# The scan's first 127 sums on VectorE, and VectorE's chains as single operations in a new order

## The chip, the core and the metric

The kernel runs on one core of one Trainium2 chip. The metric is the device time of one execution in microseconds. The core has TensorE (PE, matmuls), VectorE (DVE), ScalarE (ACT), GpSimd (POOL), and SyncE (SP), which issues all DMA transfers here. Each engine works through its own queue in order; engines meet at semaphores.

## The reference

The input x is (4, 1024, 256). Two layers follow, each inside `x = x + layernorm(layer(layernorm(x)))`.

The first layer is a gated recurrence over time, per channel and batch:

```
px = x @ W_state.T + b_state;  g = sigmoid(x @ W_gate.T + b_gate)
state = tanh(px[t] + state);   out[t] = g[t] * state        # t = 0 .. 1023
```

The second is causal attention with 16 heads of 16 (queries and keys RMS-normalised per head), then a router that picks 2 of 4 experts of one to four linear maps each with GELU or SiLU, all in float32:

```
x = x + attention(rms(x));  x = x + sum over experts of weight * expert(rms(x))
```

The tanh of step t needs the state of step t - 1, so the recurrence is 1024 dependent steps on small data: 128 partitions x 8 numbers.

## The kernel before, in words

The work is cut in time into 4 chunks of 256 steps (`NCH`) and, behind the recurrence, into 16 units (`NU`) of 256 rows each; a unit of the first chunk holds 128 time steps of two batches. Units 0 and 1 need steps 0 to 127, units 2 and 3 steps 128 to 255, and so on.

**The head.** For each of 8 half-chunks n: `xin` loads x, `hst` computes LayerNorm statistics and a reciprocal root, `hsc` scales, `htr` transposes on TensorE (4 x 2 transposes), `hcp` copies PSUM to SBUF, `hpx0` and `hpx1` are the two products (state and gate), `hout0` adds the bias (px), and `hgt` and `hout1` are the gate's tanh on ScalarE. Between these stand pieces of the weights (`wl` load, `wsh` and `wsp` split in a high and a low part, `wst` store), since float32 products are made of three products of rounded parts (`PARTS`).

**The scan.** `sadd` n adds px of step n and the state of step n - 1 on GpSimd (line 2227), `stanh` n is the tanh on ScalarE (line 1387). They alternate 1023 times. In the queues they stand between the other work of their engines: `STEPS` says how many other items come before each of them.

**A unit u.** `gl` loads the gates, `pgate` multiplies gate and state on VectorE (line 1942 for the first chunk) and waits for the last tanh of the unit's rows; `ptr` transposes, `pcp` copies, `pln` and `pu` are LayerNorms on VectorE; then `qh`, `qtr`, `qhT`, `qhl`, the products `qk` and `vm`, the norm `qrs` of queries and keys, `kh`/`kt`/`kc` and `qq`/`qt`/`qc` for keys and queries, the maxima of the scores `mxm` (TensorE) and `mxr` (VectorE, line 2026), scores and exponentials `sc`/`ex`, products with values `av`, division `mgd`, output product `wo`, norm `r3`, router `gm`/`ga`/`gex`/`gb`, experts `up`/`gel`/`dn`/`da`, last LayerNorm `fin`, store `ost`.

**The order of the work** is written out by hand in tables and the program replays it. `arrange` lists all items with an engine, a cost in us and their dependences; `Plan.sequence` orders them by `PLACES` (a place in one list for every item, 4843 of them) and puts the steps of the scan between them; `Plan.run` goes through the list, gives out buffers and PSUM banks by the costs (`PINNED` fixes some banks), and leaves one order for each engine. The costs set no time on the chip; they choose buffers, and the tables fit them.

**Dummies.** `WARM` says in front of which TensorE item how many units of two 128x128 products of the identity stand (line 1579, traced at line 1563 as `PS<-ident`); 420 units in all.

**Chains on VectorE.** An item such as `pln` (line 1945 and on), `pu`, `fin`, `r3`, `hst`, `qrs`, `kh`, `qq`, `mgd`, `ga` or `gb` is several dependent VectorE instructions. Before, they are issued one behind the other, each waiting for the one before on the semaphore `link` (`step`, `rsqrt` and `stats`, lines 1806 to 1847), with nothing of another item between. An item of VectorE is thus one piece in the order.

Of the kernel before, what the change touches and what calls it, by code (L numbers as in the profile page):

```python
# [24 lines left out]
EPS_LN = 1e-5  # L25
# [3 lines left out]
SKEW = 3e-4  # L29
FINE = 4  # L30
# [12 lines left out]
           "XF": 2, "EF": 2, "EP": 2, "W": 6, "MB": 4, "mx": 1, "MT": 1, "avbank": 1, "GG": 1}  # L43
# [9 lines left out]
RATE, IDLE = 300.0, 0.222  # L53
ISSUE = {"kst": 0.58, "vst": 0.58, "mtd": 0.73, "gl": 0.64, "kts": 0.62, "vl": 0.62, "wr": 0.6, "x1l": 0.62}
# [6 lines left out]
    "wl": (19, 2, 5, 26, 89, 58, 70, 54, 307, 111, 63, 12, 53, 190, 186, 189, 192, 195, 193, 231, 220, 249, 216, 284,  # L61
        257, 262, 235, 416, 336, 329, 322, 480),
    "cbx": (6,),
    "cqk": (108,),
    "wsp": (153, 60, 72, 474, 194, 188, 202, 210, 212, 205, 252, 255, 261, 234, 342, 335, 328, 318, 437, 523, 435, 410,
        513),
    "wsh": (191, 187, 201, 209, 211, 203, 232, 228, 260, 229, 341, 317, 313, 247, 434, 431, 423, 381, 510),
    "wst": (511, 198, 299, 238, 213, 305, 275, 256, 408, 251, 345, 556, 517, 404, 499, 524, 504, 603, 527),
    "wdd": (91, 657, 237, 147),
    "xin": (1, 17, 33, 59, 68, 88, 115, 155),  # L70
    "hst": (4, 18, 35, 61, 69, 106, 123, 164),
    "hsc": (7, 9, 10, 11, 22, 24, 30, 29, 37, 41, 42, 46, 64, 78, 79, 62, 98, 85, 102, 87, 117, 116, 135, 137, 124, 132,
        130, 144, 171, 174, 165, 173),
    "htr": (8, 13, 14, 15, 23, 25, 31, 32, 38, 43, 44, 49, 80, 81, 82, 84, 99, 101, 103, 104, 133, 134, 136, 138, 148,
        150, 151, 152, 172, 175, 176, 177),
    "hcp": (16, 48, 50, 105, 110, 143, 154, 178),
# [3 lines left out]
    "hgt": (28, 34, 36, 39, 40, 45, 47, 52, 56, 65, 66, 67, 71, 74, 77, 86, 90, 93, 94, 95, 96, 112, 131, 141, 146, 149,  # L80
# [23 lines left out]
    "pcp": (206, 224, 637, 525, 1146, 1211, 1281, 1457, 1951, 2032, 2095, 2471, 3203, 2652, 3273, 3678),  # L104
    "pln": (214, 242, 659, 538, 1147, 1217, 1305, 1470, 2009, 2066, 2124, 2529, 3227, 2673, 3287, 3701),
# [3 lines left out]
    "qtr": (226, 296, 722, 574, 1181, 1241, 1373, 1543, 2021, 2119, 2370, 2569, 3261, 2767, 3378, 3751),  # L109
    "qhT": (230, 298, 724, 577, 1209, 1245, 1378, 1567, 2026, 2176, 2383, 2586, 3269, 2784, 3408, 3761),  # L110
    "qhl": (239, 312, 731, 588, 1210, 1265, 1380, 1569, 2038, 2177, 2385, 2597, 3270, 2785, 3409, 3762),
    "qk": (240, 253, 319, 337, 732, 745, 593, 616, 1215, 1229, 1287, 1313, 1448, 1473, 1582, 1634, 2045, 2071, 2225,
        2285, 2392, 2463, 2616, 2729, 3274, 3324, 2892, 2973, 3547, 3577, 3764, 3936),
    "qkc": (245, 264, 324, 343, 737, 757, 600, 625, 1216, 1230, 1295, 1314, 1460, 1474, 1584, 1636, 2046, 2078, 2255,
        2298, 2417, 2480, 2631, 2730, 3280, 3334, 2903, 2974, 3560, 3583, 3772, 3941),
    "qred": (246, 267, 333, 344, 744, 758, 601, 654, 1221, 1235, 1296, 1315, 1463, 1476, 1633, 1640, 2047, 2079, 2257,
# [3 lines left out]
    "vst": (295, 438, 854, 776, 1282, 1437, 1553, 1866, 2249, 2488, 2620, 2910, 3488, 3317, 3612, 4175),  # L120
    "qrs": (269, 346, 759, 655, 1240, 1327, 1490, 1643, 2084, 2306, 2486, 2758, 3345, 2989, 3600, 3969),
# [6 lines left out]
    "kst": (290, 310, 392, 433, 792, 816, 691, 725, 1286, 1333, 1433, 1466, 1546, 1600, 1705, 1796, 2117, 2190, 2333,  # L128
# [2135 lines left out]
```

## Time and profile before

| | us |
|---|---|
| median of 3 runs | 1461.81 (1460.68 to 1465.23) |
| the profiled execution | 1454.77 |
| its span, first to last instruction | 1453.0 |
| TensorE matmuls busy | 1407.3 (97%) |
| VectorE busy | 1096.2 (75%) |
| ScalarE busy | 883.7 (61%) |
| GpSimd busy | 312.7 (22%) |
| mean granted TensorE clock | 0.997 of full |

Busy shares count matmuls of any kind, dummies too. Recorded durations of small instructions overlap, so an instruction's start tells more than its end. In rows of the timeline a name such as `AD<-PX` is output and input tile, `x4` a count of like instructions merged in one row, and a bracket the idle time of the engine just before with what ended it.

### The profile page before, as it was taken

The numbers are of one execution on the slowest core, as the hardware profiler recorded it, in microseconds if no ns is written. First come the engines' busy times: TensorE is split into PE (matmuls) and PEld (weight loads), VectorE is DVE, ScalarE is ACT, GpSimd is POOL, SyncE is SP. The second block draws the span as 40 slices with busy tenths as digits, with TensorE's granted clock in tenths as the row PEclk, the third lists the DMA queues.
The fourth block names the chain that finished last, engine by engine and source line by source line (L and its number), as shares of the span: only waits on it lengthen the run. The fifth ranks groups of instructions, "written<-read, shape, count | busy, mean of one in ns | idle before, by whom it ended". The sixth has DMA issues, their size and how long they took to land.

```text
span 1453.0 us, 35319 instructions
## 1 busy us (share of the span) xinstructions
PE 1407.3 (97%) x13160; PEld 1169.3 (80%) x13160; DVE 1096.2 (75%) x2916; ACT 883.7 (61%) x2262; POOL 312.7 (22%) x1146
## 2 busy tenths in 40 slices
PE   9999899999999999999999999999999999999997
PEld 6478789978997688877988689867887677986797
DVE  7858777566899877778998788788899378772544
ACT  3546577567666774776676952468322886339841
POOL 3344333332133323333333200001000100001100
PEclk9999999999999999999999999999999999999999
DMA  3547766765576657646666666676566666667453
GB/s 108 167 146 232 220 209 181 226 215 155 163 230 209 200 180 202 199 141 185 214 202 193 199 199 201 203 222 208 166 194 197 207 214 180 205 207 248 150 172 120
DMA packets 242234, 278.63 MB, mean 192 GB/s; under 512 B 35088, under 2 KB 165648, under 8 KB 241808
## 3 DMA queue, kind: packets, MB, share of 16 engines
q1 hardware_dynamic: 242064, 276.38, 62.5%
q8 instruction: 105, 1.72, 0.5%
q14 instruction: 65, 0.53, 0.1%
HBM read 234.18 MB, written 43.45 MB: 191 GB/s over the span
## 4 chain that ended last, share of the span: by engine, by line
PE 70%; DVE 14%; ACT 6%; DMA 3%; issue 3%; POOL 2%; SPq 1%; ACTq 0%; DVEq 0%; POOLq 0%
PE PS L1563 65%; PE PS L1566 3%; PE PS L1646 2%; POOL AD L2227 2%; DVE mx L2026 1%; ACT PX L1387 1%; DMA KT<-ktd 1%; DVE st L1844 1%; ACT work L1494 1%; DMA QT<-MT 1%; ACT PX L1494 1%; DVE ss L1992 1%; DVE rst L1831 1%; DVE rst L1825 1%; DVE mv L1847 0%
## 5 line engine op out<-in xcount | busy, mean ns | idle before, releaser
L1387 ACT ACTIVATE PX<-AD 128x8 f32<-128x8 f32 x1023 | 221.2, 216 | 217.6 <-POOL AD L2227 210.4
L2227 POOL TENSOR_TENSOR AD<-PX 128x8 f32<-128x8 f32 x1023 | 245.7, 240 | 499.8 <-ACT PX L1387 489.5
L2026 DVE TENSOR_REDUCE mx<-PS 128x2 f32<-128x1024 f32 (+3 forms) x256 | 254.9, 1018 | 40.4 <-PE PS L1563 39.6
L1563 PE MATMUL PS<-EP,u_e_l 128*128 128x256 f32 x1024 | 194.1, 284 | 1.3 <-issue 1.2
L1494 ACT ACTIVATE work<-PS 128x1024 f32<-128x1024 f32 (+1 forms) x199 | 182.2, 958 | 13.3 <-PE PS L1563 12.5
L1563 PE MATMUL PS<-WB,work 128*128 128x192 f32 x1024 | 180.1, 330 | 0.1
L1563 PE MATMUL PS<-work,vlx 128*32 128x256 f32 (+2 forms) x2104 | 174.8, 365 | 4.8 <-ACT work L1494 1.2
L1563 PE MATMUL PS<-EP,WB 128*128 128x256 f32 x640 | 178.8, 279 | 0.0
L1531 ACT ACTIVATE work<-PS 128x512 f32<-128x512 f32 x132 | 77.3, 595 | 160.6 <-PE PS L1563 160.1
L1563 PEld LDWEIGHTS PS<-WB,work 128*128 128x128 f32 x1024 | 164.9, 190 | 3.9 <-ACT work L1531 1.1
L1563 PEld LDWEIGHTS PS<-EP,u_e_l 128*128 128x128 f32 x1024 | 160.2, 188 | 4.5 <-issue 3.1
L1563 PE MATMUL PS<-XF,WB 128*128 128x256 f32 x576 | 161.0, 280 | 0.0
L2234 POOL TENSOR_SCALAR_AFFINE_SELECT work<-work 128x512 f32<-128x512 f32 x70 | 45.6, 659 | 454.0 <-ACT work L1494 454.0
L1563 PE MATMUL PS<-KT,QT 64*128 64x512 f32 (+3 forms) x768 | 136.2, 409 | 3.2 <-DVE mx L2026 1.6
L1563 PE MATMUL PS<-QT,KT 64*128 64x256 f32 (+1 forms) x1344 | 128.2, 303 | 5.5 <-DMA KT<-ktd 2.6
L1563 PEld LDWEIGHTS PS<-QT,KT 64*128 64x128 f32 x1344 | 93.4, 186 | 49.5 <-issue 29.1
L1563 PE MATMUL PS<-ident 128*128 128x128 f32 x840 | 123.3, 286 | 6.5 <-DVE mx L2026 2.6
L1563 PEld LDWEIGHTS PS<-work,vlx 128*32 128x32 f32 (+1 forms) x2104 | 73.7, 114 | 67.5 <-issue 33.1
L2026 DVE TENSOR_REDUCE mxb<-PS 128x2 f32<-128x768 f32 (+3 forms) x128 | 104.1, 819 | 24.4 <-PE PS L1563 23.7
L1563 PEld LDWEIGHTS PS<-ident 128*128 128x128 f32 x840 | 107.1, 194 | 18.9 <-issue 6.1
L1563 PEld LDWEIGHTS PS<-EP,WB 128*128 128x128 f32 x640 | 120.2, 188 | 0.0
L1563 PEld LDWEIGHTS PS<-XF,WB 128*128 128x128 f32 x576 | 108.3, 188 | 0.2
(201 smaller groups left out, 2600.7 us busy)
## 6 DMA issues: line engine op xcount, KB each, us to landing
KT<-ktd SPq DMA_DIRECT2D x112, 512.0 KB, 4.4
WB<-wlo_e_l SPq DMA_DIRECT2D x160, 256.0 KB, 3.6
ktd<-KTs SPq DMA_DIRECT2D x32, 512.0 KB, 4.3
WB<-wlo_e_up SPq DMA_DIRECT2D x64, 256.0 KB, 3.9
WB<-wlo_e_w SPq DMA_DIRECT2D x64, 256.0 KB, 3.8
WB<-wdn_e_down SPq DMA_DIRECT2D x64, 192.0 KB, 2.9
KT<-ktd SPq DMA_DIRECT2D x48, 256.0 KB, 3.6
KT<-ktd SPq DMA_DIRECT2D x32, 384.0 KB, 3.6
```

Source lines behind the costliest of these rows:

```text
L1387: eng.activation(cur, AD[n % 2], ACT.Tanh).then_inc(of(*key), 1)
L1494: eng.activation(pt[:, :, :, q0:L], x[:, :, :, q0:L], ACT.Exp).then_inc(of(*key), 1)
L1531: eng.activation(o, x, ACT.Gelu).then_inc(of(*key), 1)
L1563: return eng.matmul(o, l, r, start=start, stop=stop, skip_group_check=skip)
L1566: return eng.transpose(o, i, ident)
L1646: ins = eng.transpose(ps[:, p // 4, 128 * (p % 4):128 * (p % 4) + 128].bitcast(F32R), QKP[:, 2 * p:2 * p + 2, :].rearrange("p h r -> p (h ...
L1825: step(eng.reciprocal(t, t))
L1831: step(eng.reciprocal(t, t))
L1844: step(eng.bn_stats(s_[:, i, :], src[:, i, :]))
L2026: eng.tensor_reduce(o, two("mxm", *a)[:, :, 0:w], AX, ALU.max, negate=True).then_inc(of(*key), 1)
L2227: eng.tensor_tensor(AD[n % 2], PX[c % 2][:, :, :, t], PX[(n - 1) // L % 2][:, :, :, (n - 1) % L], ALU.add).then_inc(of(*key), 1)
L2234: eng.affine_select(out=p, in_=p, compare_op=ALU.is_ge, fill=0.0, base=0, pattern=[[0, 2], [0, 2], [1, 128]], channel_multiplier=-1).then_ ...
```

## The change

`sadd` 1 to 127 go to VectorE (`HERE = 128`); from 128 on they stay on GpSimd. Every chain of VectorE is listed as its single operations `("op", i, ...)`, each an item with its own place in the order; each still waits for the operation before it. `OPS` gives the number of operations ahead of the last: 1336 in all. The number of instructions stays as it was, but for small details. Scratch is made private where chains may now overlap (four sets `st2`, `mv2`, `r3`, `r4`, and the statistics' own columns for the roots). `PLACES` has 6179 entries; `STEPS`, `WARM` and `PINNED` are new as well. Some costs of the planner differ.

WARM's units by place, counted from the tables:

| before which items | before | after |
|---|---|---|
| first transposes (`htr` 0) | 32 | 4 |
| the rest of the head | 29 | 68 |
| `ptr` of unit 0 | 38 | 19 |
| the rest of unit 0 | 115 | 98 |
| unit 1 | 81 | 58 |
| units 2 to 15 | 125 | 83 |
| all | 420 | 330 |

In the order of VectorE two weight pieces (`wsh` at places 187 and 191) stand ahead of the first `pgate` (196) before, and one (`wsh` at 263, `pgate` at 265) after.

```diff
+HERE = 128
+OWN = ("pln", "pu", "fin", "r3")
+OPS = {"pln": 11, "pu": 12, "fin": 11, "r3": 8, "ga": 6, "gb": 12, "qrs": 7, "kh": 3, "qq": 1, "mgd": 1, "hst": 9}
...
+RELOAD = 0.08
...
+    def chain(key, costs, us, *after, last=(), take=None, first=(), at=None):
+
+        hold = (len(costs) if at is None else at)
+        prev = [("op", 0, key[0], key[1] - 4)] if key[0] in OWN and key[1] >= 4 else []
+        for i, cost in enumerate(costs):
+            mine = take if i == hold else None
+            if i:
+                add("dve", ("op", i, *key), cost, ("op", i - 1, *key), take=mine)
+            else:
+                add("dve", ("op", 0, *key), cost, *after, seq=[*[(k[2], k[3]) for k in prev], *first], take=mine)
+        add("dve", key, us, ("op", len(costs) - 1, *key), *last, take=take if hold == len(costs) else None)
...
-        add("dve", ("hst", n), 3.66, ("xin", n), seq=hold)
+        chain(("hst", n), (1.32, 0.28, *ROOT[1:]), 0.067, ("xin", n), first=hold)
...
-            add("pool", ("sadd", n), 0.245, ("stanh", n - 1), *px)
+            add(*(("dve", ("sadd", n), 0.075) if n < HERE else ("pool", ("sadd", n), 0.245)), ("stanh", n - 1), *px)
...
-        add("dve", ("pln", u), 4.12, ("pcp", u), ("xl", u))
+        chain(("pln", u), (0.66, 0.15, *ROOT, 0.62), 0.62, ("pcp", u), last=[("xl", u)])
...
-            add("pe", ("mgt", u, g), 0.2, ("avc", u, g), mode="128",
+            add("pe", ("mgt", u, g), 0.218, ("avc", u, g), mode="128",
...
             for key in plan.order["dve"]:
+                i, key = (key[1], key[2:]) if key[0] == "op" else (None, key)
                 kind, a = key[0], key[1:]
-                if kind == "cbx":
+                sig = of(*key) if i is None else of("op", i, *key)
+                if i:
+                    v.wait_ge(*done("op", i - 1, *key))
+                elif i is None and ("op", 0, *key) in plan.items:
+                    v.wait_ge(*done("op", OPS[kind] - 1, *key))
+                if kind == "sadd":
+                    n = a[0]
+                    v.wait_ge(*done("hout0", n // 128))
+                    v.wait_ge(*done("stanh", n - 1))
+                    eng.tensor_tensor(AD[n % 2], PX[0][:, :, :, n], PX[0][:, :, :, n - 1], ALU.add).then_inc(sig, 1)
+                elif kind == "cbx":
...
                 elif kind == "r3":
                     u = a[0]
-                    c, b = divmod(u, B)
-                    v.wait_ge(*done("sqs", u))
-                    rsqrt(r3, sq2, 2, (1.0 / C,), (EPS_RMS,))
-                    v.wait_ge(link, steps[0])
-                    for x in freed(key, "HA"):
-                        v.wait_ge(*x)
-                    for s in range(2):
-                        ins = eng.tensor_scalar(HA[:, s, :], rows_of(u)[:, s, :], r3[:, s:s + 1], None, ALU.mult)
-                    ins.then_inc(of(*key), 1)
+                    o = r3[:, u % 4]
+                    if i is None:
+                        for x in freed(key, "HA"):
+                            v.wait_ge(*x)
+                        for k in range(2):
+                            ins = eng.tensor_scalar(HA[:, k, :], rows_of(u)[:, k, :], o[:, k:k + 1], None, ALU.mult)
+                        ins.then_inc(sig, 1)
+                    else:
+                        if i == 0:
+                            v.wait_ge(*done("sqs", u))
+                        root(i, o, sq2, 2, (1.0 / C,), (EPS_RMS,), r3t[:, u % 4, 0], r3t[:, u % 4, 1]).then_inc(sig, 1)
```

The other chains are rewritten in the same way as `r3`; `root` holds the eight operations of `rsqrt`, one for each i.

## Rows read from the trace of the kernel before

**Rows 1.** The page: busy us by engine, and the chain that ended last.
```profile
PE 1407.3 (97%) x13160; PEld 1169.3 (80%) x13160; DVE 1096.2 (75%) x2916; ACT 883.7 (61%) x2262; POOL 312.7 (22%) x1146
...
PE 70%; DVE 14%; ACT 6%; DMA 3%; issue 3%; POOL 2%; SPq 1%; ACTq 0%; DVEq 0%; POOLq 0%
```

**Rows 2.** Windows: stretch, length, busy PE, PEld, DVE, ACT, POOL (instructions), clock, DMA.
```profile
20.00:30.00 10.00, 9.98 (x38) 5.31 (x37) 9.38 (x32) 5.88 (x27) 3.86 (x18) 1.00 0.46 132
...
60.00:80.00 20.00, 19.20 (x61) 9.51 (x60) 11.49 (x30) 10.12 (x46) 8.14 (x37) 1.00 0.62 177
80.00:100.00 20.00, 20.00 (x152) 17.61 (x151) 11.34 (x30) 8.62 (x39) 8.17 (x31) 1.00 0.56 170
...
350.00:500.00 150.00, 143.29 (x1364) 122.34 (x1364) 133.66 (x371) 103.23 (x318) 44.39 (x168) 1.00 0.66 199
...
1400.00:1453.00 53.00, 45.35 (x354) 44.96 (x353) 22.06 (x79) 14.05 (x21) 0.00 (x0) 0.96 0.47 145
```

**Rows 3.** Identity products on TensorE: the page's group, and 80 to 100 us.
```profile
L1563 PE MATMUL PS<-ident 128*128 128x128 f32 x840 | 123.3, 286 | 6.5 <-DVE mx L2026 2.6 <-POOL ident L2186 1.6 <-ACT work L1494 1.0
...
80.00:100.00 20.00, 15.71 (x141) 1.00 0.56 170
```

**Rows 4.** The chain that ended last in order of time: start, us, what.
```profile
1.58 8.94 PE PS L1563 x64
...
73.70 10.76 PE PS L1563 x28
...
1395.55 49.82 PE PS L1563 x386
```

**Rows 5.** Timeline of one step of the scan: start, us, engine, line, operation.
```profile
20.11 0.21 POOL L2227 TENSOR_TENSOR AD<-PX 128x8 f32<-128x8 f32 x1 [0.33 <-ACT PX L1387]
...
20.35 0.22 ACT L1387 ACTIVATE PX<-AD 128x8 f32<-128x8 f32 x1 [0.32 <-POOL AD L2227]
...
20.65 0.20 POOL L2227 TENSOR_TENSOR AD<-PX 128x8 f32<-128x8 f32 x1 [0.33 <-ACT PX L1387]
```

**Rows 6.** Groups of GpSimd, 18 to 88 us: busy us, mean ns, idle before.
```profile
L2227 POOL TENSOR_TENSOR AD<-PX 128x8 f32<-128x8 f32 x126 | 27.3, 217 | 52.3 <-ACT PX L1387 42.1 <-ACT PX L1384 10.2
```

**Rows 7.** Timeline of VectorE: a chain's end, and the next chain's first two operations.
```profile
187.72 0.16 DVE L1978 TENSOR_TENSOR tv<-tv,ru 128x2 f32<-128x2 f32 x1
187.80 0.16 DVE L1817 TENSOR_SCALAR rsx<-sq 128x2 f32<-128x2 f32 x1
188.00 0.17 DVE L1821 TENSOR_SCALAR r<-rsx 128x2 int32<-128x2 int32 x1
```

**Rows 8.** Timeline of VectorE around the first pgate (L1942).
```profile
87.25 0.43 DVE L1861 CAST u_e_up<-work 128x512 fp32r<-128x512 f32 x1 [4.72 <-DMA work<-in_L_ffn_e_up]
...
90.67 0.43 DVE L1861 CAST u_e_up<-work 128x512 fp32r<-128x512 f32 x1 [2.26 <-DMA work<-in_L_ffn_e_up]
91.13 0.69 DVE L1867 TENSOR_TENSOR WB<-work,u_e_up 128x512 fp32r<-128x512 f32 x1
91.74 0.75 DVE L1942 SCALAR_TENSOR_TENSOR G<-G,PX 128x256 f32<-128x256 f32 x2
```

**Rows 9.** Groups of VectorE by form, 18 to 88 us.
```profile
L1913 DVE COPY work<-PS 128x1024 f32<-128x1024 f32 x7 | 8.4, 1219 | 1.0 <-PE PS L1566 1.0
L1844 DVE BATCH_NORM_STATS2 st<-UU 128x6 f32<-128x256 f32 x24 | 8.4, 411 | 1.7 <-DMA UU<-in_L_attn_x 1.7
L1927 DVE TENSOR_SCALAR work<-PS,bx 128x512 f32<-128x512 f32 x8 | 5.6, 746 | 8.6 <-PE PS L1563 8.6
...
L1927 DVE TENSOR_SCALAR PX<-PS,bx 128x512 f32<-128x512 f32 x6 | 4.2, 746 | 0.6 <-PE PS L1563 0.6
```

**Rows 10.** Window of VectorE alone: length, busy us.
```profile
18.00:88.00 70.00, 50.78 (x154) 1.00 0.45 130
```

**Rows 11.** Windows of TensorE: busy us, granted clock.
```profile
640.00:660.00 20.00, 17.35 (x188) 1.00 0.55 172
660.00:680.00 20.00, 19.58 (x199) 0.91 0.48 144
```

More of the change, by code:

```diff
@@ L555, in __init__ @@
     def __init__(self):
-        self.items, self.after, self.queue = {}, {}, set()
+        self.items, self.after, self.queue, self.fresh = {}, {}, set(), set()
     def add(self, engine, key, us, *after, seq=(), take=None, mode=None, kb=0.0):
@@ L662, in run @@
                     t = max(t, t1)
+                if k in self.fresh and after == k[0]:
+                    us += RELOAD
                 us *= clock(t)
@@ L852, in arrange @@
                 take = {"P2": (("mxr", u, i),), "MB": (("mxr", u, i),)}
+                if not k0:
+                    P.fresh.add(("mxm", u, i))
                 if i == 0:
@@ L962, in arrange @@
         dma(("x1l", u), 256, ("x1st", u), take={"XR": (("fin", u),)})
-        add("dve", ("fin", u), 4.11, ("da", u, "e3_out"), ("x1l", u))
+        chain(("fin", u), (0.66, 0.15, *ROOT, 0.62), 0.62, ("da", u, "e3_out"), last=[("x1l", u)])
         dma(("ost", u), 256, ("fin", u))
@@ L1895, in _ @@
                     n = a[0]
-                    c, s = divmod(n, 2)
-                    v.wait_ge(*done("xin", n))
-                    m_ = mv.rearrange("p (b s) k -> p s b k", s=2)[:, s]
-                    stats(half(n), st.rearrange("p (b s) k -> p s b k", s=2)[:, s], m_)
-                    rsqrt(r1[:, 4 * s:4 * s + 4], m_[:, :, 1], 4, (1.0,), (EPS_LN,), key)
+                    c, h = divmod(n, 2)
+                    m_, s_ = (x.rearrange("p (b s) k -> p s b k", s=2)[:, h] for x in (mv, st))
+                    if i == 0:
+                        v.wait_ge(*done("xin", n))
+                        for k in range(4):
+                            ins = eng.bn_stats(s_[:, k, :], half(n)[:, k, :])
+                    elif i == 1:
+                        for k in range(4):
+                            ins = eng.bn_aggr(m_[:, k, :], s_[:, k, :])
+                    else:
+                        ins = root(7 if i is None else i - 2, r1[:, 4 * h:4 * h + 4], m_[:, :, 1], 4, (1.0,), (EPS_LN,),
+                                   s_[:, :, 0], s_[:, :, 1])
+                    ins.then_inc(sig, 1)
                 elif kind == "hsc":
@@ L1959, in _ @@
-                    v.wait_ge(*done("xl", u))
-                    v.wait_ge(link, steps[0])
-                    eng.tensor_tensor(xr, xr, Ub, ALU.add).then_inc(of(*key), 1)
+                    b = u % B
+                    ti, xr, Ub = 2 * b, XR[place[("xl", u), "XR"]], rows_of(u)
+                    m_, s_, o = mv[:, ti:ti + 2, :], st[:, ti:ti + 2, :], r1[:, ti:ti + 2]
+                    if i is None:
+                        v.wait_ge(*done("xl", u))
+                        eng.tensor_tensor(xr, xr, Ub, ALU.add).then_inc(sig, 1)
+                    elif i == 0:
+                        v.wait_ge(*done("pcp", u))
+                        for k in range(2):
+                            ins = eng.bn_stats(s_[:, k, :], Ub[:, k, :])
+                        ins.then_inc(sig, 1)
+                    elif i == 1:
+                        for k in range(2):
+                            ins = eng.bn_aggr(m_[:, k, :], s_[:, k, :])
+                        ins.then_inc(sig, 1)
+                    elif i < 10:
+                        root(i - 2, o, m_[:, :, 1], 2, (1.0,), (4.0 * EPS_LN,), s_[:, 0, 0:2], s_[:, 1, 0:2]).then_inc(sig, 1)
+                    else:
+                        for k in range(2):
+                            ins = eng.tensor_scalar(Ub[:, k, :], Ub[:, k, :], m_[:, k, 0:1], o[:, k:k + 1], ALU.subtract, ALU.mult)
+                        ins.then_inc(sig, 1)
@@ L1972, in _ @@
-                    for i in range(2):
-                        step(eng.tensor_scalar(rows_of(u)[:, i, :], xr[:, i, :], m_[:, i, 0:1], ru[:, b, 0, i:i + 1],
-                                               ALU.subtract, ALU.mult))
-                    t_ = tv[:, ti:ti + 2]
-                    step(eng.scalar_tensor_tensor(t_, m_[:, :, 1], EPS_LN, ru[:, b, 0], ALU.add, ALU.mult))
-                    v.wait_ge(link, steps[0])
-                    eng.tensor_tensor(t_, t_, ru[:, b, 1], ALU.mult).then_inc(of(*key), 1)
+                    b = u % B
@@ new lines, in _ @@
+                    ti, xr, Ub = 2 * b, XR[place[("xl", u), "XR"]], rows_of(u)
+                    m_, s_, t_, o = mv[:, ti:ti + 2, :], st[:, ti:ti + 2, :], tv[:, ti:ti + 2], ru[:, b]
+                    if i is None:
+                        eng.tensor_tensor(t_, t_, o[:, 1], ALU.mult).then_inc(sig, 1)
+                    elif i == 0:
+                        v.wait_ge(*done("pln", u))
+                        for k in range(2):
+                            ins = eng.bn_stats(s_[:, k, :], xr[:, k, :])
+                        ins.then_inc(sig, 1)
+                    elif i == 1:
+                        for k in range(2):
+                            ins = eng.bn_aggr(m_[:, k, :], s_[:, k, :])
+                        ins.then_inc(sig, 1)
+                    elif i < 10:
+                        root(i - 2, o.rearrange("p k s -> p (k s)"), m_[:, :, 1], 4, (1.0, 1.0 + EPS_RMS), (EPS_LN, EPS_RMS * EPS_LN),
+                             s_[:, 0, 0:4], s_[:, 1, 0:4]).then_inc(sig, 1)
+                    elif i == 10:
+                        for k in range(2):
+                            ins = eng.tensor_scalar(Ub[:, k, :], xr[:, k, :], m_[:, k, 0:1], o[:, 0, k:k + 1], ALU.subtract, ALU.mult)
+                        ins.then_inc(sig, 1)
+                    else:
+                        eng.scalar_tensor_tensor(t_, m_[:, :, 1], EPS_LN, o[:, 0], ALU.add, ALU.mult).then_inc(sig, 1)
@@ L2016, in _ @@
-                    v.wait_ge(link, steps[0])
-                    eng.tensor_tensor(QKP[:, :, low:low + 16], x, QKP[:, :, 0:16].bitcast(F32), ALU.subtract).then_inc(of(*key), 1)
+                    if i is None:
+                        ins = eng.tensor_tensor(QKP[:, :, low:low + 16], x, QKP[:, :, 0:16].bitcast(F32), ALU.subtract)
+                    elif kind == "kh" and i == 0:
+                        v.wait_ge(*done("qkc", u, h))
+                        v.wait_ge(*done("qrs", u))
+                        ins = eng.tensor_tensor(q3, q3, rqk[:, h, :].unsqueeze(2).to_broadcast([128, 32, 16]), ALU.mult)
+                    elif kind == "kh" and i == 1:
+                        v.wait_ge(*done("cqk", 0))
+                        ins = eng.tensor_tensor(q4, q4, qkw.unsqueeze(2).to_broadcast([128, 2, 16, 16]), ALU.mult)
+                    else:
+                        if kind == "qq":
+                            v.wait_ge(*done("kh", u, h))
+                        v.wait_ge(*done("consts"))
+                        for f in freed(("op", i, *key), "QKP"):
+                            v.wait_ge(*f)
+                        ins = eng.tensor_copy(pair, x.unsqueeze(2).to_broadcast([128, 16, 2, 16]))
@@ L2018, in _ @@
+                    ins.then_inc(sig, 1)
                 elif kind == "mxr":
@@ L2108, in _ @@
-                    v.wait_ge(link, steps[0])
-                    for i in range(4):
-                        pi = pr[:, :, i:i + 1].to_broadcast([128, 2, 4])
-                        step(eng.tensor_tensor(cmp_[:, :, i, :], pr, pi, ALU.is_gt))
-                        step(eng.tensor_tensor(eq[:, :, i, :], pr, pi, ALU.is_equal))
-                    v.wait_ge(*done("consts"))
-                    v.wait_ge(link, steps[0])
-                    step(eng.tensor_tensor(eq.rearrange("p t i j -> p t (i j)"), eq.rearrange("p t i j -> p t (i j)"),
-                                           lower.rearrange("p i j -> p (i j)").unsqueeze(1).to_broadcast([128, 2, 16]), ALU.mult))
@@ L2134, in _ @@
+                    ins.then_inc(sig, 1)
                 elif kind == "si":
```

474 lines of the change are left out of this document (244 added, 230 removed), and 790 rows, old and new, of tables (PINNED, PLACES, STEPS, WARM).

## The prediction

> **What bounds the kernel now.** First the busy shares: TensorE's matmuls cover 1407.3 of 1453.0 us, 45.7 are idle; VectorE has 1096.2, and the chain that ended last runs through TensorE for 70% and VectorE for 14% [rows 1]. Next the windows: TensorE is full in every stretch while VectorE is at 94% at 20 to 30 us, 57% at 60 to 100 and 89% at 350 to 500 [rows 2]. A full TensorE is not a working one here. The kernel fills waits that it foresees with dummy products of the identity (table WARM, two matmuls per unit): 840 in all, and 80 to 100 us is 15.71 us of identity work, mostly these, at 15.71 / 141 = 0.111 us each, 0.223 per unit [rows 3] (the 286 ns of the group are recorded ends that overlap). WARM's 420 units are 94 us. So the time is TensorE's real work plus dummies plus idle, and a change of order can only take from the last two.
>
> The chain in order of time shows where they cost [rows 4]. 64 dummies stand at 1.58 to 10.52 us, before the first transposes: those lie under the first load and statistics, and cost nothing. The head (transposes and px products of all eight half-chunks) ends at 73.70 + 10.76 = 84.5 us. The tail behind the last matmul (1395.55 + 49.82 = 1445.4 us) is one serial VectorE chain; no step of the change shortens a serial chain.
>
> **The change, part by part.**
>
> *127 sums from GpSimd to VectorE.* A step of the scan is a GpSimd sum and a ScalarE tanh, 0.53 us from sum to sum (20.11 to 20.65); sum to tanh is 0.24 [rows 5]. 126 sums fell in 18 to 88 us, mean 217 ns [rows 6]: 70 / 126 = 0.55 per step, about 88 us for the 127th. On VectorE, two small dependent operations follow at 0.20 and a small one lasts 0.16 to 0.17 [rows 7], against 0.20 on GpSimd. I take 0.49 per step (bounds 0.44 and 0.53): 127 x 0.49 = 62 us, which alone would end at 80.
>
> But VectorE serves its queue in order. Beside one sum (0.08 of its time, [rows 7]) a step leaves it 0.49 - 0.08 = 0.41. A longer item delays the scan by its excess: an instruction's successor starts 0.08 before its recorded end (91.13 + 0.69 against 91.74, [rows 8]), so 7 copies occupy 1.22 - 0.08 = 1.14 each, excess 0.73 x 7 = 5.1; 7 pairs of hout0, 2 x (0.746 - 0.08) = 1.33, excess 0.92 x 7 = 6.4; 6 groups of four bn_stats, 4 x (0.411 - 0.08) = 1.32, excess 0.91 x 6 = 5.5 [rows 9]. Together 17: the 127th sum comes at 18 + 62 + 17 = 97 us, a mean step of 0.62, 9 us later than before.
>
> *Unit 0.* Its first product on VectorE (pgate) ran at 91.74, not at 88: two weight pieces stood before it and VectorE waited 4.72 and 2.26 us for their loads [rows 8]. In the new order one piece stands before it. By the queue the start moves from 92 to some 97. By the tables: dummies in the head after the first transposes go from 29 to 68 units (+39 x 0.223 = +8.7 us), before unit 0's transposes from 38 to 19 (-4.2). That is +4.5, or 96: two workings agree that **unit 0 starts some 5 us later**. I take +4.5; bounds -11 (steps of 0.49 throughout, end at 80) and +19 (below).
>
> *The other dummies.* Unit 0 behind its start 115 to 98, unit 1 81 to 58: -40 units, -8.9 us. Units 2 to 15, 125 to 83: -42, -9.4 us. The 28 taken away before the first transposes save nothing. By the tables: 8.7 - 4.2 - 8.9 - 9.4 = **-13.8 us**. A dummy stands for a foreseen wait, so the table says what the order was laid out to save; bounds: -13.8, and 0 if the waits stay and show as idle.
>
> *Chains as single operations.* 1336 operations of VectorE (LayerNorm, root, router, head normalisation) keep their number, their duration and their dependences, but others may stand between them. A dependent small operation follows at 0.20 (187.80 to 188.00), an independent one at 0.08 (187.72 to 187.80) [rows 7]: 0.12 us is free behind each. Some 60 per unit are small: 16 x 60 x 0.12 = 115 us of VectorE, less 127 x 0.08 = 10 for the sums. Little of this reaches TensorE directly, which has the work of other units beside it; the shorter waits are in the dummies already. On idle that no dummy fills (45.7 less 7.6 at the end, and much of it at the start) I take -3, bounds 0 and -12. A chain that is cut open also ends later when a reduction of 1.2 us gets in; that is among the waits below. The exact costs put into the planner (transposes 0.437 for 0.4, RELOAD) change only the order.
>
> *A price that no row has.* The Trainium skill, "VectorE: DVE Perf Modes", section "The DRAIN you can't avoid", says that each operation waits for the pipe to empty whether a semaphore stands between or not, and advises fewer operations rather than fewer semaphores. By that rule interleaving frees nothing. The 0.08 against 0.20 above speaks against it for small operations.
>
> *Order anew.* Moved DMA issues on SP, and more items that wait at the front of an in-order queue: now a wait of VectorE for TensorE or a load before the 127th sum also stops the scan, with ScalarE's tanh behind it and unit 0 behind that. The waits of 4.72 and 2.26 us [rows 8] are what such a misjudged place costs. I take +5 for all of these over the run, bounds 0 and +22. Fewer dummies may also lower the clock: after 640 to 660 us with 17.35 of 20 us busy the granted clock fell to 0.91 [rows 11], about 0.09 x 20 = 1.8 us; bounds 0 and +6, taken as 0.
>
> Sum: -13.8 - 3 + 5 = -12 us (rounded). The span goes from 1453.0 to 1441, the profiled execution from 1454.8 to 1443. The median of the runs shown is 7.0 above that execution; added, **1450 us**, 0.8% faster. What this kernel's measurement can tell from no change is 0.3%, 4.4 us.
>
> **Rivals.**
>
> *The front of VectorE's queue stops the scan (slower).* Place: 18 us to the 127th sum. VectorE was idle 70 - 50.8 = 19.2 us there [rows 10], apart from gaps of 0.04 inside chains waiting for TensorE and loads. If these waits come in series with the sums instead of beside them, the 127th sum is at 97 + 19 = 116 us, and all of it delays unit 0: -12 + 19 = +7, **1469**. It decides from a delay of 12 us, a 127th sum behind 109 us, a mean step of 0.72. For it: 94% of VectorE at 20 to 30 us. Against it: idle falls as the scan stretches, and at 60 to 80 us VectorE has room.
>
> *The waits stay (no change).* Dummies go, idle comes in their place: TensorE's busy time falls by 20 us, the span does not, **1461**. For it: the order only forecasts waits, and this one's unit 0 started 3.7 us behind its last sum.
>
> *VectorE's freed time counts (larger gain).* Where VectorE is at 89%, its reductions release score banks late; with 100 us less in its queue about a third of the 38.1 us of idle outside the tail goes too: -13.8 - 12 = -26, **1436**. Against it: at 350 to 500 us the idle is only 6.7 of 150 us [rows 2].
>
> *Nothing is freed between operations.* Then a sum takes 0.20 of VectorE, not 0.08: 127 x 0.12 = +15 before unit 0: -12 + 15 = +3, and the unit chains still slower by what gets in between, say **1468**. That is what the skill's rule above would make of this kernel.
>
> **How the numbers follow.** Forecast 0.42, larger gain 0.15, waits stay 0.16, stopped scan 0.23, nothing freed 0.04. Faster by over 0.3%: 0.42 + 0.15 = 0.57 and a little of the third, 0.58. Slower: 0.27 less the part of the rival that ends within 0.3%, 0.26. Within 0.3%: 0.16. The range must reach the larger gain and the stopped scan with some width behind each: 1431 to 1471; the forecast's own is 1441 to 1457.
>
> **What would show it.** Right: no GpSimd sum before about 97 us; the 127th VectorE sum at 92 to 104, with a step of about 0.49 where no long item stands; the first pgate at 94 to 104 against 91.74; 660 identity dummies instead of 840; TensorE busy near 1387; small operations at 0.08 behind an unrelated one; VectorE's busy time below 1096 in spite of the sums. The -18.3 us of units 0 to 15 would show as units 0 and 1 taking 9 us less from first pgate to last output, and as the end coming 12 us earlier though unit 0 starts later. Wrong: the 127th sum behind 109 us, idle of VectorE for TensorE or loads with ScalarE's tanh waiting behind it; or TensorE idle above 55 us.

## The result, and the profile after

| us | before | after |
|---|---|---|
| median of 4 runs each | 1461.24 (1460.29 to 1465.23) | 1443.38 (1440.38 to 1444.5) |
| the profiled execution | 1454.77 | 1443.33 |
| its span | 1453.0 | 1441.6 |

The ratio after to before is 0.9869 [0.9846, 0.9893], 1.3% faster. A second set of runs of the same two kernels, on another chip, gave 0.9887 [0.9865, 0.9908] (medians 1448.73 and 1465.26). The span fell by 11.4 us, the median by 17.9 (16.5 in the second set). The two differ because the profiled execution of before is an unusually fast one: at 1454.77 it lies below all timed executions of before (lowest 1460.29). What the traces of before and after show, 11.4 us, is thus rather too small for the gain.

The page of the kernel after, for [rows 1] and the two groups that changed:
```profile
PE 1393.8 (97%) x12980; PEld 1157.5 (80%) x12980; DVE 1077.9 (75%) x3043; ACT 883.4 (61%) x2264; POOL 291.2 (20%) x1019
...
PE 73%; DVE 11%; ACT 7%; DMA 3%; issue 3%; POOL 2%; SPq 1%; ACTq 0%; DVEq 0%
...
L2379 POOL TENSOR_TENSOR AD<-PX 128x8 f32<-128x8 f32 x896 | 223.0, 249 | 532.1 <-ACT PX L1469 532.0
...
L1645 PE MATMUL PS<-ident 128*128 128x128 f32 x660 | 99.2, 293 | 4.7 <-POOL ident L2338 1.6
```
VectorE is busy for 18.3 us less although it has 127 sums more. TensorE has 180 products fewer, all of them dummies (660 for the 840 of [rows 3]); the real ones are the same 12,320 (12,980 - 660 and 13,160 - 840). It is idle for 1441.6 - 1393.8 = 47.8 us, before 45.7.

The tile AD (the sums) and the first pgates of the kernel after: duration min/median/max in ns, first and last start:
```profile
L2379 POOL TENSOR_TENSOR AD<-PX x896: 194/201/1262, 96.3 to 793.5; 128x8 f32<-128x8 f32 x180
L1962 DVE TENSOR_TENSOR AD<-PX x127: 153/174/179, 18.5 to 95.7; 128x8 f32<-128x8 f32 x127
...
L2062 DVE SCALAR_TENSOR_TENSOR G<-G,PX x8: 411/418/434, 96.4 to 198.6; 128x256 f32<-128x256 f32 x8
```
The 127th sum starts at 95.7, the first pgate at 96.4, 4.7 behind the 91.74 of [rows 8]. The mean step is (95.7 - 18.5) / 126 = 0.61.

Windows of the kernel after, columns as in [rows 2]:
```profile
20.00:30.00 10.00, 10.00 (x83) 9.28 (x83) 6.38 (x41) 5.24 (x24) 0.00 (x0) 1.00 0.06 20
60.00:80.00 20.00, 18.44 (x56) 8.73 (x55) 18.12 (x84) 9.97 (x45) 0.00 (x0) 1.00 0.55 153
80.00:100.00 20.00, 18.81 (x96) 12.22 (x95) 13.05 (x46) 9.94 (x45) 1.77 (x7) 1.00 0.47 135
100.00:120.00 20.00, 15.74 (x112) 14.72 (x112) 17.52 (x68) 10.32 (x45) 7.08 (x30) 0.91 0.44 133
140.00:180.00 40.00, 36.13 (x375) 30.73 (x374) 25.77 (x68) 23.56 (x102) 15.59 (x59) 0.79 0.74 213
350.00:500.00 150.00, 143.38 (x1376) 122.90 (x1375) 127.22 (x369) 103.38 (x307) 40.66 (x150) 0.99 0.66 197
```
VectorE's full stretch has moved from 20 to 30 us (94% before, 64% now) to 60 to 80 us (57% before, 91% now). At 350 to 500 us VectorE is busy for 6.4 us less (133.66 before). Behind 100 us two stretches show a lower granted clock.

**Where the time came from.** Dummies blur the picture, so the two kernels are compared at equal progress: the products that have no identity operand, counted from the start. Such a count is a window of TensorE less the same window of the identity tile (that tile's rows hold transposes too, whose number did not change). Before, 250 to 1400 us, TensorE alone and then the identity tile:
```profile
250.00:1400.00 1150.00, 1126.46 (x11023) 1.00 0.64 197
...
250.00:1400.00 1150.00, 97.45 (x580) 1.00 0.64 197
```
(11,023 - 580 = 10,443.) The kernel after did the same 10,443 products between 254.9 and 1388.8 us; the same two windows:
```profile
254.90:1388.80 1133.90, 1113.85 (x10935) 1.00 0.65 199
...
254.90:1388.80 1133.90, 81.25 (x492) 1.00 0.65 199
```

| before has done, at | after has done as many at | after minus before |
|---|---|---|
| 1065 products, 250 us | 254.9 | +4.9 |
| 1957, 350 us | 353.8 | +3.8 |
| 3181, 500 us | 498.2 | -1.8 |
| 4904, 700 us | 690.2 | -9.8 |
| 6747, 900 us | 895.3 | -4.7 |
| 8523, 1100 us | 1091.3 | -8.7 |
| 10005, 1250 us | 1238.9 | -11.1 |
| 11506, 1400 us | 1388.8 | -11.2 |

The kernel after starts unit 0 4.7 us late and is still 4.9 us late at 250 us; behind that it gains 1150 - 1133.9 = 16.1 us. Of these, 3.5 are idle time of TensorE (1150 - 1126.46 = 23.5, and 1133.9 - 1113.85 = 20.1). The other 12.6 are busy time, with 88 identity products fewer; at the 0.111 us of [rows 3] those are 9.8. The tail gives another 0.2 us.

Units 0 and 1 themselves end later than 250 us. SyncE's issue of the later of their two stores, before and after:
```profile
363.24 0.43 SPq L1363 DMA_DIRECT2D out<-UU  x1
```
```profile
364.49 0.43 SPq L1445 DMA_DIRECT2D out<-UU  x1
```
From first pgate to this store it is 363.24 - 91.74 = 271.5 us before and 364.49 - 96.38 = 268.1 after, 3.4 us less.

### The profile page after: what moved, and what is told of

The parts are those of the page before. It is cut to its first block, busy times and chain, and to the rows that moved or that the text cites. A ratio compares the mean times of both kernels' runs of the same rounds, so it can differ in the third digit from the quotient of the medians.

```text
span 1441.6 us, 34990 instructions
## 1 busy us (share of the span) xinstructions
PE 1393.8 (97%) x12980; PEld 1157.5 (80%) x12980; DVE 1077.9 (75%) x3043; ACT 883.4 (61%) x2264; POOL 291.2 (20%) x1019
## 4 chain that ended last, share of the span: by engine, by line
PE 73%; DVE 11%; ACT 7%; DMA 3%; issue 3%; POOL 2%; SPq 1%; ACTq 0%; DVEq 0%
PE PS L1645 67%; PE PS L1648 3%; PE PS L1728 2%; ACT PX L1469 2%; POOL AD L2379 2%; DVE mx L2165 2%; ACT work L1576 1%; DMA KT<-ktd 1%; DVE AD L1962 1%; DMA WB<-wlo_e_w 1%; DVE st L2013 1%; DVE UU L2026 1%; ACT PX L1576 1%; DVE mxb L2165 0%; DMA WB<-wdn_e_down 0%
## 5 line engine op out<-in xcount | busy, mean ns | idle before, releaser
L2379 POOL TENSOR_TENSOR AD<-PX 128x8 f32<-128x8 f32 x896 | 223.0, 249 | 532.1 <-ACT PX L1469 532.0
L1576 ACT ACTIVATE work<-PS 128x1024 f32<-128x1024 f32 x199 | 183.3, 958 | 17.0 <-PE PS L1645 15.8
L1645 PEld LDWEIGHTS PS<-QT,KT 64*128 64x128 f32 x1344 | 94.5, 186 | 52.5 <-issue 36.7
L2165 DVE TENSOR_REDUCE mxb<-PS 128x2 f32<-128x256 f32 (+3 forms) x128 | 103.8, 817 | 12.8 <-PE PS L1645 12.7
L1645 PE MATMUL PS<-ident 128*128 128x128 f32 x660 | 99.2, 293 | 4.7 <-POOL ident L2338 1.6
L1645 PE MATMUL PS<-XF,u_e_w 128*128 128x256 f32 x512 | 101.2, 287 | 0.5 <-DMA WB<-wlo_e_w 0.3
```

The lines of the kernel that those rows point to most:

```text
L1576: eng.activation(pt[:, :, :, q0:L], x[:, :, :, q0:L], ACT.Exp).then_inc(of(*key), 1)
L1645: return eng.matmul(o, l, r, start=start, stop=stop, skip_group_check=skip)
L2165: eng.tensor_reduce(o, two("mxm", *a)[:, :, 0:w], AX, ALU.max, negate=True).then_inc(of(*key), 1)
L2379: eng.tensor_tensor(AD[n % 2], PX[c % 2][:, :, :, t], PX[(n - 1) // L % 2][:, :, :, (n - 1) % L], ALU.add).then_inc(of(*key), 1)
```

## The experiments

Each ratio is to the kernel before on the same chip, with its 95% interval. Experiments 1 to 4 ran on one chip, 5, 6, 10 and 11 on another, and 7 to 9 and 12 on a third; the kernel after ran beside 5, 6, 10 and 11 only. "Us against the kernel after" is the ratio divided by the 0.9887 of the second set, less 1, times 1449; with the intervals of both ratios it is good to some 4 or 5 us. In the cuts of code, `...` marks what is left out.

**1. The sums back on GpSimd, all else as after.**
```diff
...
+    sums = [("sadd", n) for n in range(1, 128)]
+    P.order["dve"] = [k for k in P.order["dve"] if k not in set(sums)]
+    i = P.order["pool"].index(("consts",)) + 1
+    P.order["pool"][i:i] = sums
...
```


> The kernel after with its first 127 sums taken out of VectorE's order and put first in GpSimd's; all else, the dummies too, as after. Theory (the sums on VectorE cost time in the head, the gain is in the units): steps go from 0.46 to 0.53 us where nothing blocks, but no long VectorE item stops them, so the 127th sum comes at about 88 in place of 96 us and unit 0 starts up to 7 us earlier: 1437 to 1441 us against after's 1443. Rival (the sums on VectorE are what the change gains by): the sums on GpSimd give the gain back, 1450 us or more.

Measured: 1448.24, ratio 0.9884 [0.986, 0.9908], that is the kernel after again. The page, the sums, the group of sums from 18 to 93.5 us, and the first pgates:
```profile
PE 1394.8 (96%) x12980; PEld 1159.1 (80%) x12980; DVE 1063.4 (73%) x2916; ACT 882.6 (61%) x2264; POOL 316.1 (22%) x1146
...
L2384 POOL TENSOR_TENSOR AD<-PX x1023: 193/199/1284, 19.3 to 801.6; 128x8 f32<-128x8 f32 x171
...
L2384 POOL TENSOR_TENSOR AD<-PX 128x8 f32<-128x8 f32 x127 | 28.0, 221 | 57.6 <-ACT PX L1474 46.4 <-ACT PX L1471 11.2
...
L2067 DVE SCALAR_TENSOR_TENSOR G<-G,PX x8: 413/418/432, 94.3 to 196.7; 128x256 f32<-128x256 f32 x8
```
The 127th sum comes at 93.4 and not at the 88 that was expected: in this order a step takes (93.4 - 19.3) / 126 = 0.59 us on GpSimd too, against 0.61 on VectorE. Unit 0 starts 2.1 us sooner and nothing comes of it. In the order of the kernel after, the change's headline, the sums on VectorE, is worth nothing, to within some 5 us (this ratio and the 0.9887 of the other chip each have 0.2%); neither expectation held. With the same 2916 instructions as before VectorE is busy for 1063.4 instead of 1096.2 us: 32.8 us are freed with single operations between others. Experiment 2 gives the same size with nothing changed but the grouping.

**2. The chains whole, all else as after.** Each chain stands in one piece where its last operation stood.
```diff
...
+        if ("op", 0, *k) in P.items:
+            out += [("op", i, *k) for i in range(OPS[k[0]])]
+        out.append(k)
...
```


> The kernel after with every VectorE chain again in one piece, at the place of its last operation; the sums stay on VectorE, and the order of all else and the dummies stay as after. Theory (the gain is the 0.12 us behind each small dependent operation, used by other work): in the head 7 chains of about 3.7 us now stop the scan, 7 x 3.3 = 23 us less what was stopped by their bn_stats already (5), so the 127th sum is at about 114 us, and the units lose some 5 more: 1463 to 1470 us. Rival (an operation costs VectorE the same whatever stands between, the gain is the new order alone): 1443 to 1446 us.

Measured: 1595.27, ratio 1.0886 [1.0854, 1.0919]; the 127th sum at 113.6 as expected, 18 us later than in the kernel after, but the whole is 146 us slower than it, most of it in the units, where 5 were expected. Its page:
```profile
PE 1450.3 (91%) x12980; PEld 1196.1 (75%) x12980; DVE 1114.6 (70%) x3043; ACT 885.9 (56%) x2264; POOL 280.7 (18%) x1019
```
VectorE is busy for 1114.6 us, with the same 3043 instructions as the kernel after with its 1077.9: 36.7 us are freed by taking the chains apart. This run puts every chain's start late, so its time prices a bad order and not the cutting alone. Experiments 6 to 9 do it the other way round.

**3. The kernel before with its 127 sums on VectorE.** Chains whole, order and dummies as before.
```diff
...
+    P.order["pool"] = [k for k in P.order["pool"] if k not in sums]
+    P.order["dve"] = sorted([*P.order["dve"], *sums], key=at.get)
...
```


> The kernel before with its first 127 sums on VectorE, each at its place in the old list, the chains whole as they were. Theory (sums on VectorE need the chains cut open): 7 whole chains of about 3.7 us stop the scan in the head, 62 + 12 + 7 x 3.3 = 97 us from 18 on, so the 127th sum is at about 115 us in place of 88 and unit 0 starts about 23 us later; the order behind it is not laid out for it: 1478 to 1488 us. Rival (a sum of 0.17 us in place of 0.20 is a gain by itself): 1461 us or less.

Measured: 1518.78, ratio 1.0363 [1.0337, 1.039]. The sums, and the first pgates:
```profile
L1860 DVE TENSOR_TENSOR AD<-PX x127: 159/174/179, 18.4 to 131.2; 128x8 f32<-128x8 f32 x127
...
L1952 DVE SCALAR_TENSOR_TENSOR G<-G,PX x8: 412/418/439, 144.7 to 247.5; 128x256 f32<-128x256 f32 x8
```
The 127th comes at 131.2, a mean step of 0.90, 16 us later than expected, and the first pgate at 144.7, 53 us later than before; the run is 53 us slower. So the rival "the front of VectorE's queue stops the scan" exists: it is what happens without the cut chains and an order made for them, and which of the two is missing this run doesn't tell. Experiment 7 shows the part of the head's chains.

**4. The clock held in units 0 and 1.** 29 units of dummies more, where the kernel after lets TensorE wait before its clock falls.
```diff
+HOLD = {('ptr', 0): 11, ('qk', 0, 1): 6, ('mxm', 0, 0): 3, ('mxm', 0, 2): 3, ('kt', 1, 0): 6}
...
-                    for _ in range(WARM[key]):
+                    for _ in range(WARM.get(key, 0) + HOLD.get(key, 0)):
```


> The kernel after with 29 more units of dummies in front of TensorE's items that it waited for at 102 to 105, 116 to 118 and 144 to 150 us (11 before unit 0's transposes, 6 before qk(0,1), 3 before mxm(0,0), 3 before mxm(0,2), 6 before kt(1,0)). Theory (the clock at half for 3.4 us from 105 and 13.7 us from 149 us, behind these waits, cost the time that units 0 and 1 were to gain): both stretches go, and up to half of 17 us with them: 1435 to 1439 us. Rival (units 0 and 1 are bound by VectorE's and ScalarE's chains, and TensorE at half clock only fills its waits): 1442 to 1446 us.

Measured: 1449.2, ratio 0.9896 [0.9868, 0.9923]. Fine windows of TensorE in the kernel after, busy us and granted clock:
```profile
104.00:108.00 4.00, 2.96 (x14) 0.61 0.69 213
...
148.00:152.00 4.00, 2.58 (x32) 0.66 0.85 238
152.00:156.00 4.00, 3.47 (x44) 0.50 0.70 199
156.00:160.00 4.00, 4.00 (x32) 0.50 0.98 246
160.00:164.00 4.00, 4.00 (x31) 0.63 0.40 114
```
The first 250 us of its TensorE and its identity tile:
```profile
0.00:250.00 250.00, 229.98 (x1659) 0.96 0.58 173
...
0.00:250.00 250.00, 88.72 (x630) 0.96 0.58 173
```
Two longer windows of the kernel with the clock held, and its first 250 us in the same way:
```profile
100.00:120.00 20.00, 16.31 (x136) 1.00 0.46 146
140.00:180.00 40.00, 36.53 (x421) 0.96 0.77 216
...
0.00:250.00 250.00, 230.97 (x1715) 0.99 0.59 172
...
0.00:250.00 250.00, 92.96 (x688) 0.99 0.59 172
```
The clock is back (1.00 for 0.91, 0.96 for 0.79), and at 250 us the kernel has done 1715 - 688 = 1027 products, against 1659 - 630 = 1029 in the kernel after. So TensorE at half clock (the 1.2 GHz level) fills waits here that it would have had anyway, as the rival said. That it is the chains through VectorE and ScalarE that set units 0 and 1, the rival's reason, is what is left and was not tested by itself.

**5. The kernel after again**, on one chip with the kernels of experiments 6, 10 and 11.

> The kernel after, unchanged, beside its variants on one chip and as their measure. Every theory: 0.985 to 0.989 of before.

Measured: 1448.73, ratio 0.9887 [0.9865, 0.9908]; the base of the differences below.

**6 to 9. Operations together** (6 all seven kinds; 7, 8 and 9 the parts of the table). The operations of the named chains stand together at the place of the first; the last keeps its own place. Order of everything else, dummies and banks as after.
```diff
...
+        if k[0] == "op" and k[2] in TOGETHER:
+            if k[1] == 0:
+                out += [("op", i, *k[2:]) for i in range(OPS[k[2]])]
...
```


> The kernel after in which the operations ahead of the last one of the chains pln, pu, fin, r3, qrs, hst and ga stand together again, at the place of the first; the last operation keeps its place, the sums stay on VectorE. (The run with whole chains at the place of the last operation also made each chain start late, 1595 us; this one leaves the start.) Theory (other work between dependent operations frees VectorE time that counts): hst's 6 roots hold the scan 6 x 1.5 = 9 us more, the units lose some 5 to 10: 1.01 to 1.02 of after, 1458 to 1470 us. Rival (the cuts matter only in that the new order needs each chain's parts at their times; 422 of 1336 operations have anything behind them before the next): within 0.3% of after in the units, the head's 9 us hidden by nothing: 1.005.

> The kernel after with only the head's 8 statistics chains (hst) together again ahead of their last operation. All seven kinds together cost 1.046 / 0.989, some 83 us; 0.12 us behind each of the 292 operations that these chains had something behind would be 35. Theory A (the cost is freed time lost, by number): 39 cuts x 0.12 = 5 us, 1450 to 1454 us at after's 1448.7. Theory B (a whole chain stands in front of what a tight order put between, and that waits, the scan first of all): the 127th sum comes at 108 us as with all kinds together, 12 us later, and all of it is kept: 1459 to 1463.

> The kernel after with only the 16 last LayerNorms (fin) together again ahead of their last operation; between their parts stand 766 other operations, more than in all other chains together, and nothing but the store waits for them. Theory A (by number): 63 cuts x 0.12 = 8 us. Theory B (by what waits behind): TensorE waits for VectorE's reductions behind a chain of 2.3 us, and each of the 16 costs up to its length: 15 to 35 us.

> The kernel after with the chains pln, pu, r3, qrs and ga together again ahead of their last operation; hst and fin stay cut. Theory A: 190 cuts x 0.12 = 23 us. Theory B: the rest of the 83 us, 83 - 12 - 25 = some 45 us; if the three shares add up to far more or less than 83 us, the chains hold each other's work up.

| TOGETHER | median | ratio | us against the kernel after | 127th sum |
|---|---|---|---|---|
| 6: all seven below | 1532.28 | 1.0464 [1.0438, 1.0491] | +85 | 108.1 |
| 7: `hst` | 1462.32 | 0.9986 [0.9968, 1.0003] | +14.5 | 108.5 |
| 8: `fin` | 1476.73 | 1.0082 [1.0064, 1.0099] | +29 | 96.8 |
| 9: `pln`, `pu`, `r3`, `qrs`, `ga` | 1494.8 | 1.021 [1.0195, 1.0225] | +47 | 95.4 |

Experiment 6 missed its expectation widely: 85 us where some 10 to 20 were expected. Its parts add up (14.5 + 29 + 47 = 90), and 7 and 8 are near what the theory of blocking expected (12, and 15 to 35), where the count of free gaps gave 5 and 8. For 9 the theory's 45 was only what the 83 us left, so it tests that the parts add up; the count gave 23. They are prices in this order, which was made for cut chains. How a whole chain blocks is plain in the head, where the 127th sum comes 12.8 us later (108.5 for 95.7). VectorE's timeline with `hst` together (start, us):
```profile
21.42 0.17 DVE L1936 TENSOR_SCALAR st<-mv 128x4 f32<-128x4 f32 x1
21.62 0.17 DVE L1939 TENSOR_SCALAR r<-st 128x4 int32<-128x4 int32 x1
...
22.64 0.18 DVE L1948 RECIPROCAL st<-st 128x4 f32<-128x4 f32 x1
22.74 0.15 DVE L1972 TENSOR_TENSOR AD<-PX 128x8 f32<-128x8 f32 x1
23.16 0.17 DVE L1972 TENSOR_TENSOR AD<-PX 128x8 f32<-128x8 f32 x1 [0.28 <-ACT PX L1479]
```
and in the kernel after, in a stretch with a root between the sums:
```profile
61.00 0.17 DVE L1962 TENSOR_TENSOR AD<-PX 128x8 f32<-128x8 f32 x1
61.09 0.18 DVE L1938 RECIPROCAL st<-st 128x4 f32<-128x4 f32 x1
61.30 0.17 DVE L1933 TENSOR_TENSOR r<-r,st 128x4 f32<-128x4 f32 x1
61.46 0.17 DVE L1962 TENSOR_TENSOR AD<-PX 128x8 f32<-128x8 f32 x1
61.55 0.16 DVE L1935 SCALAR_TENSOR_TENSOR st<-st,r 128x4 f32<-128x4 f32 x1
...
62.37 0.17 DVE L1962 TENSOR_TENSOR AD<-PX 128x8 f32<-128x8 f32 x1
62.46 1.40 DVE L2047 TENSOR_SCALAR work<-PS,bx 128x512 f32<-128x512 f32 x2
63.78 0.17 DVE L1962 TENSOR_TENSOR AD<-PX 128x8 f32<-128x8 f32 x1
```
Together, no sum gets in from 21.42 to 22.74. Cut, the sums keep their 0.46 while the root goes on in the gaps; a long pair still stops them (1.41 from sum to sum at 62.37). In the units a maximum of scores can stand behind the chain. TensorE's waits, total us, times, longest, in the kernel after and then with `fin` together:
```profile
PE PS L1645 <- DVE mx L2165: 5.6, 10, 1.0
```
```profile
PE PS L1655 <- DVE mx L2175: 9.8, 9, 3.7
```
One wait of 3.7 us behind a maximum is new. That line grew by 4.2 us only, though the run lost 29. Of the 38.0 us by which this profiled execution is longer (span 1479.6 against 1441.6), 20.3 are TensorE idle and 17.7 TensorE busy, with the same products, at a mean granted clock of 0.976 against 0.987: the longer waits come with a lower clock and longer products. Whether those cost time there or only fill waits, as in experiment 4, was not tried.

**10 and 11. No dummies in units 2 to 15**, in the kernel before (125 units fewer) and in the kernel after (83 fewer).
```diff
-                if key in WARM:
+                if key in WARM and (key[0][0] == "h" or key[1] < 2):
```


> The kernel before without the 125 units of dummies of units 2 to 15. Theory (a dummy fills a wait, the gain in units 2 to 8 is in the waits): the same time or up to 10 us more, with the clock at half in more places: 1.000 to 1.007 of before. Rival (the dummies themselves cost: the new order is faster there because it has 42 units less): 0.990 to 0.994 of before.

> The kernel after without the 83 units of dummies of units 2 to 15. Theory: as for before, the same or up to 8 us more than after. Rival (dummies cost): 0.993 of after, and a version faster than both.

Measured: before 1468.09, ratio 1.0018 [1.0001, 1.0034]; after 1451.68, ratio 0.9904 [0.9883, 0.9925]. Taking away 250 products and 166 products gains nothing; in before it costs 0.2%. The window of the kernel before without them, TensorE and identity tile:
```profile
250.00:1400.00 1150.00, 1104.69 (x10731) 0.98 0.65 196
...
250.00:1400.00 1150.00, 58.86 (x344) 0.98 0.65 196
```
Idle rises from 23.5 to 45.3 us, the clock falls to 0.98, and 10,387 products are done where 10,443 were. The dummies lie in waits that are there without them. It also bears on the gain: without late dummies the two kernels lie 16.4 us apart (1468.09 and 1451.68), with them 16.5 (1465.26 and 1448.73). In units 2 to 15 the kernel after is faster because its waits are shorter, not because dummies were removed.

These two traces come from one chip. The kernel after without late dummies did those 10,387 products between 253.2 and 1387.6 us, TensorE and identity tile:
```profile
253.20:1387.60 1134.40, 1095.89 (x10733) 0.99 0.66 198
...
253.20:1387.60 1134.40, 58.22 (x344) 0.99 0.66 198
```
It is 3.2 us late at 250 us and gains 1150 - 1134.4 = 15.6 us behind it: 6.8 us are less idle time of TensorE (45.3 and 38.5), 8.8 us less busy time, for as many products of either kind, at a granted clock of 0.99 against 0.98. So the new order gains without late dummies, too.

**12. 40 units of dummies fewer in the head** of the kernel after (26 before `htr` (1, 0), 14 before `htr` (2, 0)).
```diff
+HOLD = {('htr', 1, 0): -26, ('htr', 2, 0): -14}
...
-                    for _ in range(WARM[key]):
+                    for _ in range(WARM.get(key, 0) + HOLD.get(key, 0)):
```


> The kernel after without the 40 units of dummies in front of htr(1,0) and htr(2,0). Theory (a dummy fills a wait for VectorE, and the head is later by VectorE's queue, not by TensorE's dummies): the 127th sum stays at 96 us and the time within 0.3% of after. Rival (the +39 units are themselves the 8.7 us by which the head got longer): 6 to 9 us faster than after.

Measured: 1455.77, ratio 0.9931 [0.9905, 0.9958]; the 127th sum at 97.5 in an execution of span 1444.0. The scan doesn't come sooner, nor does unit 0 (first pgate at 98.2), so the head's added dummies are not what delays them, and the 6 to 9 us that the rival expected to win are excluded. Whether the run is slower than the kernel after stays open: the intervals touch, and its runs spread from 1445.75 to 1464.51.

## Why the prediction was right, and where it was not

**The sum.** Forecast -12 on the span and 1443 for the profiled execution; measured -11.4 and 1443.33. The median was forecast at 1450 by adding the 7.0 us of before; it came out at 1443.38. That offset belongs to one unusually fast execution, not to the kernel: in the second set after's median stood 3.0 above its profiled execution. By medians the change is -17.9 and -16.5 us, half again the -12 of the sum, so the close hit on the span is in part luck.

**The terms did not hit one by one; two misses cancelled.**

- *The scan, right.* 127th sum forecast at 97, measured 95.7. The unblocked step was 0.46, not 0.49; what long items cost was then 77.2 - 126 x 0.46 = 19, not 17. On GpSimd, where no item of VectorE stops the sums, the new order's scan is only 2.3 us earlier (experiment 1).
- *Unit 0 starts 4.5 us later, right:* 96.4 against 91.74. The working by the queue held. The working by the dummies (+8.7 - 4.2) gave the same number by luck: 40 of the units less, and unit 0 starts no sooner (experiment 12).
- *Units 0 and 1 give back 8.9 us, wrong.* This is the step that failed: "Unit 0 behind its start 115 to 98, unit 1 81 to 58: -40 units, -8.9 us". From first pgate to last output the two units take 3.4 us less, not the 9 that were to show it, and at 250 us the kernel is as late as unit 0 started. The dummies went and waits came in their place: TensorE is idle for 20.0 of the first 250 us (14.5 before), and its clock fell to 0.50 in stretches between 104 and 180 us. Experiment 4 shows that the clock is not the cause: held up, the progress is the same. In these two units the rival "the waits stay" was right for the most part.
- *Units 2 to 15, undersized.* Forecast -9.4 for dummies and -3 for idle. Measured -16.1 (-15.6 for the pair of experiments 10 and 11): idle -3.5 as forecast, busy time -12.6 where -9.4 was taken. The +5 for misjudged waits was put in no stage; it may be part of the miss in units 0 and 1, and behind 250 us nothing of it shows. Experiments 10 and 11 confirm that the table told of waits.
- *Freed time of VectorE, mis-sized.* "16 x 60 x 0.12 = 115 us" counted every small operation. In the order of the kernel after only 422 of the 1336 have another item ahead of their successor, 422 x 0.12 = 51 us at most, and 32.8 and 36.7 were measured (experiments 1 and 2). A sum adds (1077.9 - 1063.4) / 127 = 0.11 us, not 0.08.
- *What cutting a chain is worth* was taken at nearly nothing beyond the dummies, since free gaps seldom reach TensorE. Experiments 6 to 9 price it at 85 us in this order: a sum no longer waits for the whole chain (shown in the head), nor does a maximum of scores (shown for one wait of 3.7 us). The gain over before is about a fifth of that (11 to 18 us). Before has an order laid out for whole chains, so it did not pay the 85 us; that is argued, not shown.
- *Clock taken as 0, right in time.* It did fall in units 0 and 1, at no measured cost.

**What the signs showed.** No GpSimd sum before 96.3; 660 dummies; VectorE 1077.9, below 1096; TensorE idle 47.8, below 55: as written. Units 0 and 1 taking 9 us less: not so. TensorE busy was 1393.8, not 1387; the lower clock lengthens products, for with the clock held it is 1393.7 with 58 dummies more, 1393.7 - 58 x 0.111 = 1387 without them. A small operation 0.09 behind an unrelated one (61.46 to 61.55), and 0.21 behind the one it depends on (61.09 to 61.30), stands in the rows above.

That last pair decides the rival that nothing is freed. The Trainium skill, "VectorE: DVE Perf Modes", section "The DRAIN you can't avoid", says that the next operation does not start before the pipe is empty and that a semaphore costs nothing extra; it adds that an operation that is not held starts earlier, which the prediction left out. For operations of 2 to 8 elements per partition the trace agrees with the addition and not with the free semaphore: a wait for the result costs 0.12 us that an unrelated operation need not pay.

**Open.** How much of the gain the cutting would bring in before's own order was not tried, nor whole chains in a new order made for them, so the gain can't be split between the cut chains and the new order. Left by the experiments is this: it comes neither from the sums on VectorE nor from fewer late dummies, it lies behind 250 us, and the new order needs its chains cut. What the 29 and 47 us of experiments 8 and 9 are made of, wait by wait, isn't shown.

## What to carry to other kernels

On an engine that works through its queue in order, a chain of small dependent operations cost less here by its own time (33 to 37 us of VectorE freed) than by what stood behind it (85 us): cut it where something urgent waits, and price the cut by who waits behind the chain, not by the idle gaps. Removed dummies count as a gain only where the wait they stood for is gone too, so compare kernels by real products done at equal times. And moving a chain of dependent steps to another engine with nearly the same step (0.46 for 0.53 us) was worth nothing here, since that engine also served long items. Last, a difference of two single profiled executions (11.4 us) can be a third below that of the medians (16.5 to 17.9).

## What had not been expected of the hardware

TensorE at half clock for most of 148 to 163 us cost no time that could be measured (experiment 4). The small sum is only 0.03 us shorter on VectorE (median 174 ns, on GpSimd 201), but the round with ScalarE's tanh by 0.07. ScalarE's timeline of the kernel after, the tanh behind the sum of 61.00:
```profile
61.21 0.22 ACT L1469 ACTIVATE PX<-AD 128x8 f32<-128x8 f32 x1 [0.24 <-DVE AD L1962]
```
Sum to tanh is 0.21 against the 0.24 of [rows 5], and tanh to sum 0.25 (61.21 to 61.46) against 0.30 (20.35 to 20.65).
